# A gated layer with Toeplitz convolutions and a mixture of experts: start-up loads, context turning and small scalar steps re-ordered

## The reference, cut to what matters

```python
x = x + jnp.tanh(g_xattn[0]) * xattn(ctx, ctx, layernorm(x), ssm_kernel, D, 8)
x = x + jnp.tanh(g_ffn[0]) * ffn(layernorm(x), router_w, router_b, expert_w, expert_b, out_w, out_b)

# xattn: k = v = ctx, q = layernorm(x); 16 heads of 8 channels, sequences of 256
kv = einsum('bhil,bhjl->bijhl', k_, v_)
y  = irfft(rfft(kv, 512) * rfft(ssm_kernel, 512))[..., :256]      # a causal convolution
out = einsum('bijhl,bhil->bjhl', y + kv * D, q_)
# ffn: router logits, softmax, top 2 of 8 experts, gelu(x @ expert_w + b), weighed sum, @ out_w
```

## Time and profile before

| | us |
|---|---|
| median of 3 runs | 114.57 |
| lowest and highest | 114.37, 114.65 |
| the profiled execution: its own time | 114.24 |
| its span, first to last instruction | 112.4 |
| PE, DVE, ACT, POOL busy in it | 104.1, 89.4, 57.7, 61.8 |

### The profile page before, as it was taken

One profiled execution on the slowest core, in us unless ns is written; L12 is line 12 of the kernel. 1 busy time (PEld: TensorE's weight loads), 2 busy tenths in 40 slices (PEclk: granted clock), 3 DMA queues, 4 the chain that ended last, 5 costly groups with the idle time before them and its releaser, 6 DMA issues.

```text
span 112.4 us, 1942 instructions
## 1 busy us (share of the span) xinstructions
PE 104.1 (93%) x586; PEld 88.9 (79%) x586; DVE 89.4 (80%) x294; ACT 57.7 (51%) x145; POOL 61.8 (55%) x82
## 2 busy tenths in 40 slices
PE   4937999999999999999999999999999999999960
PEld 4928988789989977867698888887788888888930
DVE  0186799999999999999899977887289986866930
ACT  4060859076236278563669788856363344354300
POOL 4024898999999959999999999800000000000000
PEclk9995899999999999999999999999999999999997
DMA  2956999369664530002000000000000111011031
GB/s 80 271 166 177 287 374 320 121 172 222 239 202 155 167 120 3 0 13 84 0 6 0 0 0 0 0 0 0 0 0 6 47 47 47 3 47 47 0 99 47
DMA packets 10956, 10.02 MB, mean 89 GB/s; under 512 B 1306, under 2 KB 10946, under 8 KB 10946
## 3 DMA queue, kind: packets, MB, share of 16 engines
q1 hardware_dynamic: 9570, 8.85, 26.5%
q10 hardware_dynamic: 1376, 1.05, 3.1%
HBM read 8.82 MB, written 1.07 MB: 88 GB/s over the span
## 4 chain that ended last, share of the span: by engine, by line
PE 50%; DVE 22%; POOL 12%; DMA 6%; issue 4%; ACT 1%; SPq 1%; DVEq 0%; POOLq 0%
PE ring L869 11%; PE ring L871 11%; PE ring L870 11%; DVE zq_t L1054 6%; POOL zq_t L411 6%; DVE zq_t L1056 5%; DMA ctx_t<-in_ctx 4%; DVE kv_t L379 3%; PE red L810 3%; DMA dcol<-in_L_xattn_D 2%; DVE zq_t L1059 2%; DVE zq_t L1058 2%; PE red L736 2%; PE zbank L911 2%; POOL kv_t L379 2%
## 5 line engine op out<-in xcount | busy, mean ns | idle before, releaser
L1154 DVE SCALAR_TENSOR_TENSOR mix_t<-ring,ctxT_t,mix_t 128x256 f32<-128x256 f32 x53 | 25.4, 483 | 6.0 <-ACT ring L625 4.5
L625 ACT ACTIVATE ring<-ring 128x512 f32<-128x512 f32 (+1 forms) x32 | 18.1, 567 | 18.7 <-PE ring L871 18.6
L379 POOL TENSOR_TENSOR kv_t<-ctxT_t 128x320 f32<-128x320 f32 x25 | 21.5, 888 | 7.9 <-ACT ctxT_t L537 5.7
L869 PE MATMUL ring<-w_hi_t,zT_hi_t 128*128 128x512 f32 (+1 forms) x64 | 25.5, 399 | 0.0
L871 PE MATMUL ring<-w_hi_t,zT_lo_t 128*128 128x512 f32 (+1 forms) x64 | 24.7, 385 | 0.0
L870 PE MATMUL ring<-w_lo_t,zT_hi_t 128*128 128x512 f32 (+1 forms) x64 | 24.6, 384 | 0.0
L786 PE MATMUL ring<-kv_t,toep_t 128*128 128x288 f32 x64 | 21.4, 416 | 0.0
L787 PEld LDWEIGHTS ring<-kv_t,toep_t 128*128 128x128 f32 x64 | 12.2, 190 | 3.4
L871 PEld LDWEIGHTS ring<-w_hi_t,zT_lo_t 128*128 128x128 f32 x64 | 12.0, 188 | 2.5
L869 PEld LDWEIGHTS ring<-w_hi_t,zT_hi_t 128*128 128x128 f32 x64 | 12.1, 188 | 2.2
L870 PEld LDWEIGHTS ring<-w_lo_t,zT_hi_t 128*128 128x128 f32 x64 | 12.1, 189 | 2.0
(11 more groups left out here) (133 smaller groups left out, 178.8 us busy)
## 6 DMA issues: line engine op xcount, KB each, us to landing
ctx_t<-in_L_ffn_expert_w SPq DMA_DIRECT2D x8, 256.0 KB, 4.3
toep_t<-kpad_dram SPq DMA_DIRECT2D x3, 512.0 KB, 6.6
x_t<-in_x SPq DMA_DIRECT2D x8, 128.0 KB
out<-x_t SPq DMA_DIRECT2D x8, 128.0 KB
wlast_t<-in_L_ffn_expert_w SPq DMA_DIRECT2D x1, 768.0 KB, 5.9
ctx_t<-in_ctx ACTq DMA_DIRECT2D x2, 256.0 KB, 2.9
zq_t<-in_x ACTq DMA_DIRECT2D x2, 256.0 KB, 4.3
ctx_t<-in_ctx SPq DMA_DIRECT2D x2, 256.0 KB, 4.5
```

Of the source, the lines that this page charges most:

```text
L379: eng.tensor_tensor(dst, head.unsqueeze(1).to_broadcast([P, HB + 1, HD * CB]), windows(ctxT_t, g, h, HB + 1), ALU.mult).then_inc(done, 1)
L625: act.activation(y, y, ACT.Gelu_apprx_tanh).then_inc(gelu_ready, 1)
L869: pe.matmul(y, hi, whi, start=(c == 0), stop=False)
L1154: dve.scalar_tensor_tensor(out=acc, in0=block_bank(n)[:, L * e:L * (e + 1)], scalar=gate, in1=acc, op0=ALU.mult, op1=ALU.add).then_inc(mix ...
```

## The change

On **SP** D is loaded before the taps, context loads 0 and 1 follow (they were on ACT), then comes the scratch write. Context loads 2 and 3 leave their place behind it. Behind the third Toeplitz load now stand x load 2, context loads 2 and 3, and x load 3; Toeplitz loads 3 and 4 follow.

On **ACT** the queue begins with x loads 0 and 1 and the gains. The tanh stands before all copies. The four copies of group 1's context stand between `statistics(5)` and `statistics(6)`.

On **TensorE** contexts 0 and 1, then the first queries, then convolutions 0 to 4, then contexts 2 and 3, then convolution 5 and the rest. The warm-up is 16 transposes at first, 1 between contexts 0 and 1 and 10 behind context 1 (before: 12, 1, 6, 1, 5); the 5 near the end stay.

On **GpSimd** the first power comes before products 1, with its wait for VectorE's four first queries. On **VectorE** the first queries come before products 0, products 2 behind the copy of the queries, products 5 behind query products 1.

```diff
-WARM_UP = (12, 1, 6, 1, 5, 5)
+WARM_UP = (16, 1, 10, 5)
...
+            sp.dma_start(dcol[:, :], ssm_d.rearrange("(h a) -> h a", a=1)).then_inc(taps_in, 16)
             sp.dma_start(taps[:, :], ssm_kernel).then_inc(taps_in, 16)
-            sp.dma_start(dcol[:, :], ssm_d.rearrange("(h a) -> h a", a=1)).then_inc(taps_in, 16)
-
+            for i in range(2):
+                load(sp, cv, ctx_in, context_in, i)
             sp.wait_ge(taps_reversed, 1)
             sp.wait_ge(constants_ready, 1)
             sp.dma_start(scratch, kpad[:, :]).then_inc(scratch_written, 16)
-            for i in range(2, LOADS):
-                load(sp, cv, ctx_in, context_in, i)
             sp.wait_ge(scratch_written, 16)
             for i, (h, n) in enumerate(TOEP):
...
-                if i >= len(TOEP) - 3 and i < len(TOEP) - 1:
-                    load(sp, xn, x, x_in, i - len(TOEP) + 5)
+                if i == 2:
+                    load(sp, xn, x, x_in, 2)
+                    load(sp, cv, ctx_in, context_in, 2)
+                    load(sp, cv, ctx_in, context_in, 3)
+                    load(sp, xn, x, x_in, 3)
...
+            first_inverse_std()
             products(pool, 1, pool_products_ready)
-            first_inverse_std()
...
-            for i in range(2):
-                load(act, cv, ctx_in, context_in, i)
             for i in range(2):
                 load(act, xn, x, x_in, i)
...
+            act.wait_ge(gains_in, 32)
+            act.activation(tgains[:, :], gains[:, :], ACT.Tanh).then_inc(tanh_ready, 1)
             for c in range(C):
                 evacuate(ctxT, red, context_transposed, 0, c, context_evacuated)
-            act.wait_ge(gains_in, 32)
-            act.activation(tgains[:, :], gains[:, :], ACT.Tanh).then_inc(tanh_ready, 1)
             half_gains()
+            evacuate(qT, (zbank, obank), queries_transposed, 0, 0, act_queries_evacuated)
+            statistics(4)
+            statistics(5)
             for c in range(C):
                 evacuate(ctxT, red, context_transposed, 1, c, context_evacuated)
-            evacuate(qT, (zbank, obank), queries_transposed, 0, 0, act_queries_evacuated)
-            for n in range(4, 8):
-                statistics(n)
+            statistics(6)
+            statistics(7)
...
-            for i in range(LOADS):
+            for i in range(2):
                 context(i)
                 warm_up(WARM_UP[i + 1], ring[RING - 1])
             queries(0)
             queries(1)
-            for n in range(0, 15):
+            for n in range(0, 5):
+                convolve(n)
+            context(2)
+            context(3)
+            for n in range(5, 15):
                 convolve(n)
...
+            first_queries()
             products(dve, 0, dve_products_ready)
-            first_queries()
+            evacuate_queries()
             products(dve, 2, dve_products_ready)
+            query_products(0)
+            query_products(1)
             products(dve, 5, dve_products_ready)
-            evacuate_queries()
-            for n in range(0, 8):
+            for n in range(2, 8):
                 query_products(n)
```

## The result

With the change the kernel takes **114.77 us** (median of 20 runs, 114.49 to 114.97) against 114.18 us before on the same chip (20 runs, 113.30 to 115.85). The ratio is 1.0056, with a 95% interval of 1.0039 to 1.0073: slower by 0.6 us, where I had forecast 114.5, no change, with a range of 113.6 to 115.5. The profiled execution took 114.78 us, its span is 113.0 us against 112.4.

The account below looks back on a forecast made before the run. The end was taken to hang on the start of GpSimd's scales at 20.76 us. At T = 7.5 they come at 20.82, +0.06 less up to 0.15, so 114.5 us from the 114.57 median, range 113.6 to 115.5.

Parts of the forecast that it names:

- T: Landing time of the scratch write: 8.24 us before, forecast 7.5, bounded between 6.7 and about 8.5.
- Toeplitz loads and late loads: Loads SP issues from T on: x load 2 lands at T + 7.0, context load 3 at T + 8.5.
- faster, the scratch write gets out early: Rival: T = 6.7, convolution 5 at 15.8, scales 0.75 us earlier, 113.8 us; chance 0.33.
- Convolution 5: On TensorE behind context 3: starts at T + 9.1 = 16.6 us, against 16.54 before, so no gain left.
- break-even T: Scratch write landing at which convolution 5 starts as before: forecast 7.44 us.
- The scales and what follows: GpSimd's products 12 at 18.3, scales at 20.8, ScalarE's last statistics at 20.6; query product 16 follows scales by 7.5 us.
- meeting within 0.2 us: Ways to the scales by GpSimd (20.8) and ScalarE (20.6) meet; the moved copies use up ScalarE's slack and cost nothing.
- VectorE is off the path: VectorE's query product 5 at 17.5 against 18.08 before: it keeps 0.5 us, off the path.
- Small steps at nothing: Tanh before copies, power before products 1: group 0 copies end near 8.8, products 1 start near 9.5, both hidden.
- Slower, the scratch write stays where it was: Rival: T = 8.24 to 8.5, convolution 5 at 17.3 to 17.6, scales 0.8 to 1.05 later, 115.4 to 115.6; chance 0.22.
- The clock: Rival: TensorE drops to 1.2 GHz, convolutions take 1.46 instead of 0.73 us, loss of 1 to 1.5 us; chance 0.10.
- The chain isn't GpSimd's: Rival: query product 16 doesn't hang on the scales, VectorE's 0.5 us or up to 1.7 stay, 113.5; chance 0.04.

Follow-up runs that it names:

- experiment 2: Changed kernel with contexts 2 and 3 turned behind convolution 7 instead of 4, all statistics ahead of group 1's copies: 114.32 us, ratio to before 1.0005.
- experiment 6: Changed kernel with context loads 2 and 3 ahead of x load 2 instead of behind it: 115.63 us, ratio to before 1.0142.
- experiment 7: Changed kernel with VectorE's products 2 ahead of its copies of the queries: 114.70 us, ratio to before 1.0061.
- experiment 8: Changed kernel with 3 warm-ups behind context 1 instead of 10: 114.94 us, ratio to before 1.0072.
- experiment 9: Changed kernel, x loads 2, 3 behind Toeplitz load 2, contexts 2, 3 loaded behind Toeplitz load 3, turned behind convolution 9, copied behind all statistics: 114.26 us.
- experiment 10: Kernel before with only the late contexts' new place (loads, turning, group 1's copies), 12 warm-ups behind context 1: 116.27 us, ratio to before 1.0203.
- experiment 11: Kernel before with only the late contexts' new place, 36 warm-ups behind context 1: 114.77 us, ratio to before 1.0079.
- experiment 3: Changed kernel with context loads 2 and 3 back right behind the scratch write: 114.93 us, ratio to before 1.0052.
- experiment 4: Changed kernel, context loads 2, 3 behind scratch write, contexts turned behind first queries, group 1's copies before statistics, 7 warm-ups instead of 10: 113.70 us, ratio to before 0.9959.
- experiment 5: The kernel of experiment 4 with 7 warm-ups between contexts 0 and 1 instead of 1: 113.65 us, ratio to before 0.9982.
- experiment 1: Kernel before with one spare GpSimd power right ahead of the scales of group 1: 115.55 us, ratio to before 1.0079.
- experiment 12: Kernel before with the small steps alone (tanh ahead of copies, power ahead of products 1, VectorE's order): 116.56 us, ratio to before 1.0181.

## Why the prediction was wrong, point by point

**In short.** Two steps failed. The late loads were to land at T + 8.5 and landed at T + 9.07: that put convolution 5 and GpSimd's products 12 to 14 0.6 us behind before. And the path behind them was another: the sum counted the start of the scales, put VectorE off the path and its products at nothing. VectorE sets query product 16, and its products beside GpSimd's cost it up to 0.6 us each.

**T, the landing of the scratch write.** Forecast 7.5, measured 7.56: the term held, with luck. The profiles with the changed kernel's order up to Toeplitz load 0 have T = 7.56, 7.43, 7.22, 7.28, 8.00 and 7.46 (after, experiments 2, 6, 7, 8, 9), so one profile tells it to some 0.4 us. Its reason was half right. With context loads 0 and 1 still on ACT, T is 7.95 and 7.37 (experiments 10 and 11); with context loads 2 and 3 right behind the write it is 7.92, 8.10 and 7.85 (3 to 5), and with all of before's order 8.24, 8.57 and 7.89 (before, 1, 12). The means are 7.5 without context loads 2 and 3 behind the write and 8.1 with them. So what brought T down, on the mean, was that they went away. A cost of the half MB in the write's own queue doesn't show within this spread. The rule of the Trainium skill that I had weighed (DMA: Bandwidth & Descriptors, Queues, rings and completion order) would have made T near 8.5; with the context loads in the write's queue no profile has more than 8.10.

**Toeplitz loads and late loads: the mis-sized term.** x load 2 was to land at T + 7.0 and came at T + 7.56, context load 3 at T + 8.5 and came at T + 9.07. The 1.51 us between the two are my 1.55; the 0.57 us were lost ahead of them. Toeplitz load 2 landed 6.81 us behind T, against 6.31 before (14.55, T 8.24). It stands so in every kernel that has no context loads between scratch write and Toeplitz loads (T + 6.70 to T + 6.98 in experiments 2, 6 to 11), and context load 3 in all of those with the change's order at T + 9.07 to T + 9.25. With the context loads there it is T + 6.4 to T + 6.6 (experiments 1, 3, 4, 5, 12). I had taken landing times of one queue filling as a property of the loads behind it, and gave no bound to them. Read without T it is plainer: x load 2, right behind Toeplitz load 2, landed at 14.92 to 15.12 us in the seven profiles with T from 7.28 to 7.89 (after, experiments 2, 5, 7, 9, 11, 12), where before it was at 15.26. An earlier T hardly moved it, so the T + 7.0 of the sum was wrong in form and not only in size, and the rival "faster, the scratch write gets out early" was not on offer: with T at 7.28 convolution 5 still came at 17.06 (experiment 7). Why it is so is not settled: the 16 DMA engines finished Toeplitz load 2 over 1.6 us in the profile after and over 0.7 before, but no run changed that by itself.

**Convolution 5.** T + 9.1 = 16.6 was forecast, 17.17 measured, 0.54 behind the landing of load 3, as the 0.6 for turning and handing over said. So the sum with the right landing is 7.56 + 9.07 + 0.54 = 17.17. The break-even T would have been 6.9, not 7.44, hardly above my lower bound of 6.7: with this term known, "slower" was the likeliest case. And as the landing doesn't follow T, no T that was seen would have reached it (convolution 5 at 17.06 to 17.64 in experiments 7, 8 and 11, 16.54 before).

**The scales and what follows: the right distances, the wrong path.** Forecast 18.3, 20.8 and 20.6 for products 12, scales and the last statistics; measured 18.88, 21.38 and 21.07. Each is late by what its landing was late, and the scales stand 4.21 behind convolution 5 (4.22 before). The "meeting within 0.2 us" of the two ways held too (0.3), as experiments 3 and 6 show from the other side. But I took the 7.5 us from the scales to query product 16 for the length of their chain. It held as a number (7.53 and 7.53) because VectorE was as late as the scales; the chain itself is 7.1 us long (experiments 1 and 6). By it alone query product 16 would have come near 28.5, not at 28.91.

**VectorE is off the path: wrong.** I wrote that it keeps 0.5 us (query product 5 at 17.5 instead of 18.08). It came at 18.38. The row that I needed is VectorE's products 22 of before, ending right at query product 16, and the chain of waits, which names VectorE from 13.09 to the end of the stretch. What was missing is the cost of VectorE's products.

Up to query product 5: products 2 and 5 ran in 0.89 us for both before, ahead of the copies of the queries; moved behind them, they stand in the string and took 1.04 and 1.12, beside GpSimd's products. And the first queries were turned at 10.45, though VectorE had them ready at 9.44, because ten warm-ups took 2.22 us. So VectorE started its copies 1.56 us earlier (11.53 against 13.09), needed 1.84 us more from there to query product 5 (6.85 against 5.01), and was 0.28 late. By its rows convolution 5 let it start there near 18.1 (0.94 us behind, as in experiments 7, 8 and 11), so its own order set this point.

From query product 5 to 16: VectorE has no wait in this stretch in nine profiles. Where products 11 took 0.47 to 0.54 us, the stretch is 10.06 to 10.19 (before, experiments 4, 5, 12); where they took 1.16 or 1.17, it is 10.81 or 10.82 (7, 8, 10, 11); after, with 0.90, it is 10.53. That is the other 0.34 of the loss. It comes from convolution 5: with it late, GpSimd's products 12 to 14 run until 21.3 instead of 20.67 and meet VectorE's products 11. In experiment 11 it accounts for the loss: with products 11 at 0.54 query product 16 would have been at 28.2 by VectorE and at 28.4 by the scales, instead of 28.85. In experiment 7 it takes back what the better order gave.

What is shown and what isn't: that the late contexts' place is enough for the loss is shown by experiment 11, which has it alone, and that it is needed by 2, 4 and 9, which take it away and leave VectorE's order. That it acts through products 11 is read from the rows of these nine profiles; no run moved that collision by itself. The 0.28 us of VectorE's own order are of the one profile after.

**Small steps at nothing.** Copies of group 0 ended at 10.29 instead of 8.8 and products 1 began at 10.43 instead of 9.5: both hidden, as said. The cover is the load order. Without it they and VectorE's order together cost 2.3 us (experiment 12).

**The rivals.** "Slower, the scratch write stays where it was" had the size and the place (convolution 5 at 17.3, late loads behind T), with the wrong member late. The clock did not slow a convolution in the changed kernel, whose runs are all at 0.985 or more and whose convolutions took 0.73 us in the profile; only the ten warm-ups took 2.22 us there instead of the 1.25 of experiment 3. Its mechanism is real, with the price I had given (1.44 us a convolution, experiment 10). "The chain isn't GpSimd's" was set aside because copies end at 28.20 right ahead of 28.29. It had the path right and the sign wrong: the row shows a tie and not a cause, and VectorE had lost time, not kept it.

## What to carry to other kernels

Read the chain of waits over the stretch that a change touches, and look for an engine that runs without a wait right up to the point where another hands over: two chains that meet within 0.1 us both have to be sped up, and either can lose. Delay one of them alone, as experiment 1 does: if less than the whole delay arrives, that chain had time to spare. Where a sum has a break-even within 0.1 us of its value, each of its terms needs a bound: a landing time taken from a queue in another state of filling is one with half a us of doubt. When loads are moved, ask what else waits for their buffers: here turning the contexts later gave 1.7 us and lost it again, as the next loads go to the same tiles.

## What the runs showed of the hardware

- A product of VectorE (two operands in SBUF, 128x320) took 0.47 to 0.63 us when it got in ahead of GpSimd's or just as one ended, and 0.76 to 1.17 when it came while one of GpSimd's ran; query products, with one operand from PSUM, kept their 0.41. The first case costs GpSimd instead: its product beside VectorE's two at 11.41 before took 1.42 us, that beside VectorE's at 14.88 in experiment 5 took 1.14, where GpSimd's alone take 0.83. The Trainium skill (SBUF — State Buffer, Who interferes with whom) states such a lock for VectorE instructions with two SBUF inputs, and these rows agree. I had priced the moved products as if they were free.
- The windows view of the changed kernel gives 1.00 as the granted clock from 8 to 10.3 us, yet ten transposes there took 2.22 us, 0.22 each, where they took 1.25 us in the run of experiment 3. The first clock record of that trace lies at 10.4 us; in that stretch the durations say more than the clock column.
- With the same code the low clock came in some runs and not in others: experiment 4 at 0.977 to 0.985 in four of eleven runs (the one of 119.25 apart), and these took some 0.9 us more (114.12 to 114.61 against 113.06 to 113.86). The kernel before falls into groups too: beside experiments 5, 9 and 10 five of its 23 runs took 113.35 to 113.50 at 0.994 to 0.996, one 113.88 at 0.994, ten 114.00 to 114.28 at 1.00, and seven 114.27 to 114.65 at 0.979 to 0.983. Its profile (0.979) is of the last group; none of before is of the fastest.
